# A four-layer graph network: the copy of the inputs dropped, degrees looked up on chip, work moved between stages and engines

## The reference

```python
# layer 0, gcn: degrees are counted over src
w   = deg[src]**-0.5 * edge_weight * deg[dst]**-0.5        # 0 where src == dst or a degree is 0
out = segment_sum(w * h[dst], src) + h / deg               # second term 0 where deg is 0
# layer 1, two SAGE convolutions, means over the edges of a dst
h1  = relu(mean(h[src]  -> dst) @ W1_l.T + b1 + h  @ W1_r.T)
out = relu(mean(h1[src] -> dst) @ W2_l.T + b2 + h1 @ W2_r.T)
# layer 2, messages and an update, mean over the edges of a dst
msg = relu([h[src], h[dst], edge_attr] @ mW1 + mb1) @ mW2 + mb2
upd = relu([h, mean(msg -> dst)] @ uW1 + ub1) @ uW2 + ub2 + h
out = layernorm(upd) * gamma + beta
# layer 3, mean over the edges of a src
out = relu(h @ W_self.T + b_self + where(count > 0, mean(h[dst] -> src) @ W_neighbor.T + b_neighbor, 0))
```

## Time and profile before

| what | value |
|---|---|
| median of 3 runs | 4984.89 us (4975.8 to 4988.58) |
| profiled execution, its own time | 4997.06 us |
| span of its trace | 4995.3 us |
| busy, share of the span | TensorE 75%, VectorE 72%, ScalarE 73%, GpSimd 73% |
| DMA | 915 MB, 183 GB/s over the span |
| mean granted clock of TensorE | 0.897 |

### The profile page before, as it was taken

The page is one execution under the profiler, slowest core; times in us unless marked ns, Lnnn a source line. Parts: engine busy times, 40 slices in busy tenths (PEclk is TensorE's granted clock), DMA queues, the critical chain, the costliest instruction groups (busy, mean ns, idle before and its releaser), DMA issues. The chain is left out here.

```text
span 4995.3 us, 76977 instructions
## 1 busy us (share of the span) xinstructions
PE 3727.3 (75%) x21984; PEld 2954.3 (59%) x22295; DVE 3616.6 (72%) x12174; ACT 3634.7 (73%) x9165; POOL 3637.0 (73%) x2968
## 2 busy tenths in 40 slices
PE   6537777787778778888878888889688875666664
PEld 4326655565666666767755666666576764544543
DVE  7648777797889986777767777777687885655443
ACT  0048878899878878888788888788687874766564
POOL 7777665545788867888767777775688876777777
PEclk9868989999899899999989999999899997877777
DMA  8999988896767766776668989997565654333332
GB/s 251 320 291 299 266 239 241 241 266 166 183 157 165 162 128 157 161 158 156 139 188 216 267 234 256 250 245 193 136 143 136 146 121 99 98 96 96 96 95 66
DMA packets 935298, 915.09 MB, mean 183 GB/s; under 512 B 86536, under 2 KB 718662, under 8 KB 934870
## 3 DMA queue, kind: packets, MB, share of 16 engines
q1 hardware_dynamic: 612124, 617.22, 38.7%
q0 software_dynamic: 216384, 232.05, 27.0%
q10 hardware_dynamic: 106362, 60.87, 4.4%
HBM read 390.36 MB, written 575.02 MB: 193 GB/s over the span
## 5 line engine op out<-in xcount | busy, mean ns | idle before, releaser
L1247 POOL DMA_INDIRECT node<-sage_comb,leadd x392 | 637.2, 1626 | 172.7 <-DMA node<-sage_comb,leadd 90.4
L462 ACT ACTIVATE dense_h<-dense_x,dense_n_shift,dense_n_rstd 128x128 f32<-128x128 f32 x1304 | 533.8, 486 | 54.0 <-DVE dense_n_shift L451 53.5
L468 PE MATMUL dense_p<-ident,dense_h 128*128 128x128 f32 x1956 | 328.1, 294 | 320.1 <-ACT dense_h L462 313.7
L1247 POOL DMA_INDIRECT node<-gcn_comb,leads x196 | 323.0, 1648 | 300.1 <-issue 235.7
L468 PEld LDWEIGHTS dense_p<-ident,dense_h 128*128 128x128 f32 x1956 | 231.4, 148 | 424.3 <-ACT dense_h L462 405.3
L1247 POOL DMA_INDIRECT sums<-mlp_same,leadh x196 | 322.5, 1645 | 129.5 <-issue 73.1
L478 PE MATMUL dense_p<-wT,dense_hT 128*128 128x128 f32 x2608 | 365.7, 286 | 25.3 <-ACT dense_hT L1076 10.0
L1247 POOL DMA_INDIRECT sums<-mean_comb,leads x196 | 322.1, 1643 | 84.3 <-DMA sums<-mean_comb,leads 43.6
L478 PEld LDWEIGHTS dense_p<-wT,dense_hT 128*128 128x128 f32 x2608 | 367.5, 204 | 26.7 <-issue 11.3
L1076 ACT ACTIVATE dense_hT<-dense_p 128x512 f32<-128x512 f32 x489 | 284.9, 589 | 29.4 <-PE dense_p L468 28.4
L462 ACT ACTIVATE dense_h<-dense_y,dense_n_shift,dense_n_rstd 128x128 f32<-128x128 f32 x652 | 268.0, 487 | 35.2 <-DVE dense_n_shift L451 33.6
(11 more groups left out here) (314 smaller groups left out, 13094.2 us busy)
## 6 DMA issues: line engine op xcount, KB each, us to landing
node<-b SPq DMA_DIRECT2D x196, 512.0 KB
sums<-zero_row SPq DMA_DIRECT2D x392, 256.0 KB
node<-zero_row ACTq DMA_DIRECT2D x49, 1152.0 KB
node<-in_x SPq DMA_DIRECT2D x195, 256.0 KB
dense_x<-in_x SPq DMA_DIRECT2D x163, 256.0 KB
out<-dense_y SPq DMA_DIRECT2D x163, 256.0 KB, 3.6
x_dst<-xd SPq DMA_DIRECT2D x49, 256.0 KB, 5.8
gcn_x<-x_dst SPq DMA_DIRECT2D x49, 256.0 KB, 6.4
```

The lines of the kernel that those rows point to most:

```text
L462: tiles(lambda t: nc.scalar.activation(out[:, t, :], x[:, t, :], func, bias=b.sh[:, t:t + 1], scale=b.rs[:, t:t + 1])).then_inc(done, 1)
L468: return tiles(lambda t: nc.tensor.transpose(ps[:, t * P:(t + 1) * P], x[:, t, :], ident))
L1247: pool.indirect_dma_start(table, bass.IndirectOffsetOnAxis(ap=leads[:, i * G + c, t:t + 1], axis=0), e.comb[c][:, t, :], None, element_off ...
```

## The change

The copy of x into the node table goes, and with it the x columns (the table is 400 floats wide and `AG` is 0). In place of x_dst, preparation gathers x[src] (196 gathers) and stores it to x_src, from which sage1 loads linearly; it also issues the first two rounds of gcn's gathers of x[dst] (40), straight into gcn's tiles (`gather_x`); gcn issues the other 156 itself. The table small goes with its gathers. The degrees at the other end of each edge are looked up from the histogram instead: the counts are split into two f16 parts (`split_counts`), the high parts of the node numbers of a chunk become one-hot columns (`shape_rows`), TensorE multiplies them with the counts (`look_rows`), and VectorE picks the right low part with an accumulating comparison (`pick_count`). The look-up of the src degree at each edge's dst is in preparation, in 49 rounds behind the histogram; that of the dst counts is in gcn, in two new steps each on two more PSUM banks.

Other edits: three lasting dense streams of 62 chunks and one extra of 10 in gcn (`PARTS`, `MORE`); the keys of sage1 and sage2 are loaded by DMA (get_keys) and not spread on TensorE; in sage1 the comparison of lead, with another mask, serves as match too, and keep multiplies by 1/count on VectorE; sums is zeroed in full rows in sage1 and sage2 and not in mlp; the comparisons of mean's first half carry the weight, so its match leaves out two of six operations; the residual of a dense chunk in gcn and in mean, two of its norms in mlp and one in mean move to VectorE (`RES`, `NORMS`); the last dense sum and its relu become one operation. The due times in `TIMES` are new for all stages but final. The core of the diff:

```diff
-AG, W1, W2, WT = 128, 272, 400, 528
-PARTS = (55, 54, 54)
-MORE = (11, 11, 11)
+PARTS = (62, 62, 62)
+MORE = (10,)
...
+def norm_rows(nc, dve, done, at, i, name, b, out, x):
+    tiles(lambda t: nc.vector.tensor_scalar(out[:, t, :], x[:, t, :], b.st[:, t, 1:2], b.rs[:, t:t + 1],
+                                            ALU.subtract, ALU.mult)).then_inc(done, 1)
...
-        self.small = dram("small", (NT, 2), F32)
+        self.hi_rows = dram("hi_rows", (NCH * T, P), F16)
-        self.xd = edge_rows("x_dst")
+        self.xs = edge_rows("x_src")
...
+def gather_x(pool, pace, k, ea, inp, n, i, c):
+    for t in (2 * n, 2 * n + 1):
+        gather(pool, pace, ea.x[c][i % 2][:, t, :], inp["x"], k.gdst[:, i * G + c, t:t + 1], ea.x_in[c][i % 2])
...
+def split_counts(nc, counts, hist, signal, dve, n):
+    nc.vector.tensor_copy(counts[q, 0, :, :], hist[q, :, 0:LOW]).then_inc(signal, 1)
+    nc.vector.tensor_tensor(counts[q, 1, :, :], hist[q, :, 0:LOW], counts[q, 0, :, :], ALU.subtract).then_inc(signal, 1)
...
+def shape_rows(nc, ea, hot, row):
+    for u in range(U):
+        last = nc.vector.tensor_scalar(hot[q, u, :], row[q, :], ea.place[q, u:u + 1], None, ALU.is_equal)
+    return last
...
+def look_rows(nc, ps, hot, counts, t):
+    terms = [(u, part) for u in range(U) for part in range(2)]
+    for n, (u, part) in enumerate(terms):
+        last = nc.tensor.matmul(ps[:, 0:LOW], hot[q, u, t * P:(t + 1) * P], counts[q, part, u, :],
+                                start=(n == 0), stop=(n == len(terms) - 1))
+    return last
...
+def pick_count(nc, ea, ps, picked, i, c, t, to):
+    return nc.vector.scalar_tensor_tensor(out=picked[:, :], in0=ea.iota[:, :], scalar=ea.low_d[:, i * G + c, t:t + 1],
+                                          in1=ps[:, 0:LOW], op0=ALU.is_equal, op1=ALU.mult, accum_out=to)
...
-def copy_rows(eng, table, x, filled, n):
-    a, b = n * CH, min((n + 1) * CH, N)
-    eng.dma_start(table[a:b, 0:D], x[a:b, :]).then_inc(filled, 16)
...
-                tiles(lambda t: gather(pool, pace, xd[c][:, t, :], inp["x"], k.gdst[:, i * G + c, t:t + 1], gathered[c]))
+                tiles(lambda t: gather(pool, pace, xs[c][:, t, :], inp["x"], k.gsrc[:, i * G + c, t:t + 1], gathered[c]))
+            pool.wait_ge(dst_in, 48)
+            for i in range(2):
+                for c in range(G):
+                    for n in range(2):
+                        gather_x(pool, pace, k, ea, inp, n, i, c)
...
-                sp.dma_start(chunk_rows(tb.xd, i, c), flat(xd[c][:, :, :])).then_inc(kept[c], 16)
+                sp.dma_start(chunk_rows(tb.xs, i, c), flat(xs[c][:, :, :])).then_inc(kept[c], 16)
...
-                fill_rows(act, tb.node, AG, W1, k.zero[:, 0:WS], filled, c)
+                fill_rows(act, tb.node, 0, W1, k.zero[:, 0:W1], filled, c)
+            fill_tail(act, tb.sums, 0, 2 * D, k.zero[:, :], filled)
...
-            act.dma_start(tb.small.rearrange("(b h l) k -> h b (l k)", h=HIGH, l=LOW),
-                          val[q, :, :, :].rearrange("h b l k -> h b (l k)")).then_inc(table_out, 16)
...
+            split_counts(nc, counts_s, hist[:, 0, :, :], split, dve, 0)
+            split_counts(nc, ea.counts_d, hist[:, 1, :, :], split, dve, 1)
+            dve.wait_ge(hrow_in, 16)
+            shape_rows(nc, ea, hot[0], hrow[:, 0:CH]).then_inc(shaped, 1)
+            for m in range(NCH):
+                if m + 1 < NCH:
+                    shape_rows(nc, ea, hot[(m + 1) % S], hrow[:, (m + 1) * CH:(m + 2) * CH]).then_inc(shaped, 1)
+                for t in range(T):
+                    dve.wait_ge(looked, m * T + t + 1)
+                    if m > 0:
+                        dve.wait_ge(picks, (m - 1) * T + t + 1)
+                    pick_count(nc, ea, hist[:, t // 2, t % 2, :], picked[t], m // G, m % G, t, deg[:, m, t:t + 1]).then_inc(picks, 1)
...
+            nc.vector.tensor_tensor(rec[:, :, DISD:DISD + T], rroot[:, :, :], ind[:, :, :], ALU.mult).then_inc(table_step, 1)
+            nc.vector.tensor_tensor(rec[:, :, EW:EW + T], rec[:, :, EW:EW + T], rec[:, :, DISD:DISD + T], ALU.mult)
...
+            pe.wait_ge(split, 4)
+            for m in range(NCH):
+                pe.wait_ge(shaped, m + 1)
+                for t in range(T):
+                    if m > 0:
+                        pe.wait_ge(picks, (m - 1) * T + t + 1)
+                    look_rows(nc, hist[:, t // 2, t % 2, :], hot[m % S], counts_s, t).then_inc(looked, 1)
...
-RES = {"gcn": TENSOR, "sage1": TENSOR, "sage2": VECTOR, "mlp": VECTOR, "mean": TENSOR}
+RES = {"gcn": VECTOR, "sage1": TENSOR, "sage2": VECTOR, "mlp": VECTOR, "mean": VECTOR}
+NORMS = {"gcn": (), "sage1": (), "sage2": (), "mlp": ("h1_", "t_"), "mean": ("h1_",)}
...
-            nc.vector.tensor_tensor(flat(y[:, :, :]), p[:, :], flat(h[:, :, :]), ALU.add).then_inc(done, 1)
+            nc.vector.scalar_tensor_tensor(out=flat(y[:, :, :]), in0=flat(h[:, :, :]), scalar=0.0, in1=p[:, :],
+                                           op0=ALU.max, op1=ALU.add).then_inc(done, 1)
...
-    if e.whole:
+    if e.whole and first:
...
-            in1=k.one[:, :], op0=ALU.is_equal, op1=ALU.mult, accum_out=seen[:, u:u + 1])
+            in1=k.one[:, :] if weight is None else weight[:, U + u:U + u + 1].to_broadcast([P, HALF]), op0=ALU.is_equal, op1=ALU.mult, accum_out=seen[:, u:u + 1])
...
-            in1=k.mask[:, t % U, :], op0=ALU.is_equal, op1=ALU.mult,
+            in1=(k.mask if mask is None else mask)[:, t % U, :], op0=ALU.is_equal, op1=ALU.mult,
...
+        nodes = ([Node("shape", VECTOR, 750, after=(("get_h", 1, 0),)),
+                  Node("get_h", SYNC, 450, after=(("shape", 0, 0),), main=False)]
+                 + [n for h in range(U) for n in (Node(f"look{h}", TENSOR, 1550, take="look"), Node(f"pick{h}", VECTOR, 1050, give="look"))]
+                 + ln("x_", after=(("fetch1", 1, 0),))
+                 + [Node("y", VECTOR, 1060, after=(("put_y", 1, 0),)), Node("put_y", SYNC, 450, after=(("y", 0, 0),), main=False)]
+                 + fetch_nodes(2, "y", 1, begun=1)
...
-                    if q < FILLS:
-                        fill_rows(sp, tb.node, W1, WT, k.b12[:, :], e.filled, i * G + c, 4 * q, 4)
-                    elif ((i * G + c) * FILLS + q - FILLS) * CH < N:
-                        copy_rows(sp, tb.node, inp["x"], e.filled, (i * G + c) * FILLS + q - FILLS)
+                    fill_rows(sp, tb.node, W1, WT, k.b12[:, :], e.filled, i * G + c, 2 * q, 2)
...
+                    gather_x(pool, pace, k, ea, inp, int(name[5:]), i + 1, c)
-                    add_pair(pool, pace, e, plan, tb.node, k.leads, name, i, c, AG)
-            for c in L:
-                for n in range(2):
-                    pair(n, 0, c)
+                    add_pair(pool, pace, e, plan, tb.node, k.leads, name, i, c, 0)
...
-                if name == "weigh":
+                if name == "shape":
+                    shape_rows(nc, ea, hot[c], hrow[c]).then_inc(e.done[c], 1)
+                if name.startswith("pick"):
+                    for u in range(U):
+                        t = U * int(name[4:]) + u
+                        last = pick_count(nc, ea, look[u], picked[c][u], i, c, t, field(k, i, c, INVD)[:, t:t + 1])
...
+                if name.startswith("look"):
+                    for u in range(U):
+                        last = look_rows(nc, look[u], hot[c], ea.counts_d, U * int(name[4:]) + u)
+                    last.then_inc(e.done[c], 1)
...
-        nodes = ([Node("counts", VECTOR, 100, after=(("fetch1", 1, 0),)), Node("root", SCALAR, 205)]
-                 + ln("x_")
-                 + [Node("self", VECTOR, 1060, after=(("put_x1", 1, 0),)),
+        FILL = ("x_norm", "h_norm", "lead", "combine")
+        nodes = (ln("x_", after=(("get_xs", 1, 0),))
+                 + [Node("counts", VECTOR, 100, after=(("fetch1", 1, 0),)),
+                    Node("root", SCALAR, 205), Node("self", VECTOR, 1060, after=(("put_x1", 1, 0),)),
+                    Node("get_xs", SYNC, 450, after=(("self", 0, 0),), main=False),
                     Node("x1", VECTOR, 1060)]
-                    Node("spread", TENSOR, 560), Node("krow", SCALAR, 500), Node("lead", VECTOR, 2500), Node("dup", VECTOR, 110), Node("leader", VECTOR, 110),
+                    Node("lead", VECTOR, 2500, after=(("get_keys", 1, 0),)), Node("get_keys", SYNC, 450, after=(("lead", 0, 0),), main=False), Node("dup", VECTOR, 110), Node("leader", VECTOR, 110),
-                 + edge_tail(True, SCALAR, whole=True) + fill_nodes(FILL))
+                 + edge_tail(True, SCALAR, whole=True, matched=True, keep_on=VECTOR) + fill_nodes(FILL))
...
-                    fill_rows(sp, tb.sums, 0, D, k.zero[:, 0:D], e.filled, i * G + c, 4 * q, 4)
+                    fill_rows(sp, tb.sums, 0, 2 * D, k.zero[:, :], e.filled, i * G + c, 2 * q, 2)
...
+                leaders_vector(nc, dve, k, e, name, i, c, KD, SKD, count[c], dup[c], k.leadh, seen[c], k.past, 1.5)
-                if name == "match":
```

(20 more changed lines are left out.)

382 lines of the change are left out of this document (224 added, 158 removed), and 309 rows, old and new, of the table TIMES.

## The result

The changed kernel took 5058 us (median of four runs, 5045 to 5118) against 4987 before; over all runs that is 1.0165 times as long, interval 1.0123 to 1.0207, so slower by 1.2 to 2.1%. The forecast was 4950 and faster. The profiled execution took 5044.5 us, span 5042.8, 47.5 more than before's span.

A forecast was written before the change was run, and what follows sets the result against it. GpSimd's indirect transfers were taken to bound most stages, DMA then dense work gcn. Preparation +69, gcn -127 and later stages +25 sum to -33 us from 4985, about 4950 us; range 4855 to 5055.

The forecast's parts named there:

- at 205 us 81 of 196 are left: Preparation: gathers still to issue after the histogram, at today's pace; with 40 more 121, the last issued at 356 us.
- +69: Preparation: added look-ups and their tail make gcn start at about 381 us instead of 312.
- a look-up round: Preparation: one of 49 added rounds of degree look-ups on TensorE and VectorE, 3.05 us each with handshakes, 150 us in all.
- The rival of slow gathers: Preparation: gathers stay at 1.41 us through the look-ups, gcn starts at 418 us, program 4987 us; chance 0.10.
- 785 forecast: gcn: length at a VectorE share of 0.885 over 695 us of work, a change of -127 us.
- So VectorE or ScalarE decides: gcn: with DMA near 645 us and GpSimd about 590, VectorE (695 us busy) or ScalarE (538) sets the length.
- its issues (about 590 us): gcn: GpSimd's time after falling from 392 to 352 issues.
- The term +25: sage1, sage2, mlp and mean: price of taking 26 dense chunks from gcn, between nothing and 123 us.
- GpSimd's count is unchanged, so I stay near the low end: Later stages: GpSimd's unchanged issues still set their ends, so 25 us is taken from the span of nothing to 123.
- The rival of overflowing stages: Later stages: all 123 us of TensorE's excess falls at the stage ends, program 5048 us; chance 0.10.

The follow-up runs named there:

- e18b: Changed kernel with the four short key copies on VectorE put ahead of the histogram, not between two rounds; 1.0056 of the kernel before, preparation 365 us.
- e8: Changed kernel without VectorE's picks and the reciprocal behind them in gcn's look-ups; program 5068 us, gcn as long as without the edit.
- e13: Changed kernel with GpSimd's gcn order rearranged, at most one pair of gathers behind each pair of additions; 1.0136 of the kernel before, gcn 771 us.
- e11: Changed kernel with gcn's five streams adding to five separate tables, each waiting only for its own last addition; program 5031 us, gcn 772 us.
- e4: Changed kernel with 12 of 196 dense chunks left out (lasting streams of 58, not 62); 0.9998 of the kernel before, mean 56 us shorter.

## Why the prediction was wrong

**Preparation.** The step that failed is "at 205 us 81 of 196 are left": it took over the gathers' pace in the histogram, because the histogram stayed. The comparisons had stayed, but not what stands between their rounds: with four copies there the gathers went into another step, 124 were left, and the term came to +99, not +69. Moving the copies alone (e18b) takes 46 us off preparation; why one step holds and not another stays open. The rest of the working held: a look-up round took (349 - 211) / 49 = 2.8 us (forecast 3.05), the gathers behind 205 us 0.94, VectorE's tail ended 12 us ahead of forecast, and in e18b, at the old pace, the last gather is issued at 357.4 us (forecast 356). The rival of slow gathers had its end, 418 us, nearly right and its place wrong: it put them in the look-ups. By the Trainium skill's port rule (page "SBUF — State Buffer", section "SBUF: two separate sides") the two f16 comparisons of a look-up round would slow them too; no gather behind 205 us took over 1.03 us, and the measurement decides.

**gcn.** The length (785 forecast, 797 to 809 measured), VectorE's share (0.885, 0.90) and DMA's (below 0.85, 0.81) came out, the chunks nearly (41, 46). The sentence "So VectorE or ScalarE decides" was wrong all the same, so the near length was luck: e8 took 98 us off VectorE without effect, and e13 shortened gcn with the work of both unchanged. What sets gcn in its place, as far as the runs show, is GpSimd's walk through pairs of additions, their landings and the gathers between them; the forecast priced its issues (about 590 us) and no wait. The earlier trace rows and a busy share cannot tell a bound from a neighbour; the waits of GpSimd for landings could have. The Trainium skill, page "DMA: Bandwidth & Descriptors", section "Rules for kernel authors", asks that an accumulating DMA wait for the semaphore of an earlier one on the same bytes. Here the pairs, each behind such a wait, follow each other every 7.4 to 8.7 us, and e11, without the waits between streams, shows what these alone are worth: 25 to 37 us of 797 to 809.

**Later stages.** The term +25 was mis-sized, at +65. "GpSimd's count is unchanged, so I stay near the low end" assumed that the stages would share the chunks by their room, 6 to 8 more each. sage1, sage2 and mlp kept their lengths and took five, three and two; mean, last in line, got eleven, and e4 prices them. The rival of overflowing stages came nearest, with 123 us spread over the ends of all four; the overflow came at the end of one. Sizing the tail of the last stage, not an average over four, was the step to take.

The three misses, 30 + 12 + 40 us, make 82; the profile moved by +47.5 where -33 was forecast, 80.5, and final's 2 us are the difference. The medians moved by 71 us, 24 more than the profiled executions: that of the kernel before was 10 us above its median, that of the changed one 14 below, with the shortest gcn of those profiled in this order (797 us, the others up to 809). Of the other executions there is no trace.

## What to carry to other kernels

Work taken out of a stage must be followed to the last stage that can take it: the stages between keep their written order, and what they leave over falls on the end. Before an engine at 0.9 is called the bound, take some of its work away and see whether the stage gets shorter; an ordered chain of transfers can fill the same time and show as idle gaps on another engine. Where GpSimd issues transfers beside a dense run of VectorE's f16 operations, look at the duration of its instructions after every edit to that run, even one that adds nothing.
